# Layer 0 of a four-layer graph kernel: blocks of 512 query rows, four heads in turn for each tile, and layer seams worked block by block

## What is computed

```
layer 0: Q, K, V = h @ Qw + Qb, h @ Kw + Kb, h @ Vw + Vb          (8 heads)
         e[i,j,h]  = leaky_relu(S1[i, adj[i,j], h] + S2[j, adj[i,j], h], 0.2)
         out       = softmax_j(e) @ V per head, then @ Pw + Pb     (every j counts, adj picks the relation)
layer 1: hn = (h - mean(h)) / norm;  s = (hn @ w_k) @ (hn @ w_q)^T / sqrt(8)
         a  = adj * softmax(s), rows made to sum to 1;  (a + a^2/2 + a^4/6) @ hn
layer 2: Wh = h @ W;  e = leaky_relu(Wh a1 [i] + Wh a2 [j], 0.2)
         elu(softmax_j(e where adj > 0) @ Wh)
layer 3: a hyperbolic log-map summed over neighbours, then an exp-map
```

## Time and profile before

| | us |
|---|---|
| time, median of 3 executions | 1080.58 (1079.04 to 1087.63) |
| the profiled execution, its own time | 1082.16 |
| its span in the profile | 1079.9 |
| PE busy | 937.5 (87%) |
| DVE busy | 728.5 (67%) |
| POOL busy | 555.8 (51%) |
| ACT busy | 546.0 (51%) |

### The profile page before, as it was taken

One profiled execution on the slowest core, in us unless ns is written; L12 is line 12 of the kernel. 1 busy time (PEld: TensorE's weight loads), 2 busy tenths in 40 slices (PEclk: granted clock), 3 DMA queues, 4 the chain that ended last, 5 costly groups with the idle time before them and its releaser, 6 DMA issues.

```text
span 1079.9 us, 14479 instructions
## 1 busy us (share of the span) xinstructions
PE 937.5 (87%) x5239; PEld 336.0 (31%) x5239; DVE 728.5 (67%) x1145; ACT 546.0 (51%) x943; POOL 555.8 (51%) x658
## 2 busy tenths in 40 slices
PE   1996999999999999999996599999667939999970
PEld 1762222222222222222223522333262334555430
DVE  3145777777778777777774567411328667999987
ACT  0374666666665666656660076100100137899970
POOL 2006788898889888888870000000000007799962
PEclk8566999999999999999997579999857965999995
DMA  9472002021211121120000000000000000000000
GB/s 196 64 156 80 12 21 75 21 71 33 66 38 59 33 67 35 28 73 22 22 21 1 0 1 1 1 1 1 1 0 39 1 1 0 1 1 1 1 0 19
DMA packets 24940, 34.05 MB, mean 32 GB/s; under 512 B 16219, under 2 KB 16363, under 8 KB 23718
## 3 DMA queue, kind: packets, MB, share of 16 engines
q1 hardware_dynamic: 22566, 24.75, 7.9%
q0 software_dynamic: 2304, 8.39, 4.4%
HBM read 40.22 MB, written 1.30 MB: 38 GB/s over the span
## 4 chain that ended last, share of the span: by engine, by line
PE 72%; DVE 16%; issue 4%; DMA 3%; SPq 2%; ACT 1%; POOL 1%; DVEq 0%; ACTq 0%; POOLq 0%
PE ps L1074 22%; PE ps L1084 11%; PE ps L1181 8%; PE ps L1061 5%; DVE big L411 4%; PE ps L1053 4%; PE ps L1215 3%; PE ps L1155 3%; PE ps L1251 3%; DVE big L724 2%; DMA big<-in_L_gnn_Pw_dram 2%; DVE big L408 2%; PE ps L1145 2%; PE ps L938 1%; PE ps L1223 1%
## 5 line engine op out<-in xcount | busy, mean ns | idle before, releaser
L530 DVE COPY_PREDICATED big<-mask,ps 128x512 f32<-128x512 uint8 x512 | 338.2, 724 | 115.2 <-PE ps L1061 107.6
L368 POOL TENSOR_SCALAR big<-big 128x512 f32<-128x512 f32 x512 | 356.3, 713 | 72.5 <-PE ps L1084 72.2
L851 ACT ACTIVATE ps<-ps 128x512 f32<-128x512 f32 x512 | 266.8, 582 | 167.1 <-PE ps L1053 167.1
L1074 PE MATMUL ps<-big 128*64 128x512 f32 x1024 | 258.9, 613 | 0.0
L380 POOL TENSOR_TENSOR big<-big 128x512 f32<-128x512 f32 x40 | 67.3, 1684 | 342.1 <-ACT big L911 342.1
L1084 PE MATMUL ps<-big 128*32 128x512 f32 x1024 | 136.5, 605 | 0.0
L1053 PE MATMUL ps<-op_r,op_l 18*128 18x512 bf16 x512 | 110.3, 386 | 8.4 <-DMA op_r<-split_scratch 7.1
L1074 PEld LDWEIGHTS ps<-big 128*64 128x64 f32 x1024 | 58.6, 136 | 135.7 <-issue 98.4
L1251 PE MATMUL ps<-big 66*128 66x512 f32 x160 | 86.1, 668 | 2.2 <-DVE big L697 1.3
L411 DVE TENSOR_TENSOR big<-big,mask 128x512 f32<-128x512 f32 (+1 forms) x72 | 65.8, 933 | 12.8 <-ACT big L871 11.5
L1061 PE MATMUL ps<-op_r,op_l 9*128 9x512 bf16 x512 | 70.7, 390 | 2.0 <-ACT ps L851 2.0
(11 more groups left out here) (235 smaller groups left out, 1137.1 us busy)
## 6 DMA issues: line engine op xcount, KB each, us to landing
big<-max_scratch SPq DMA_DIRECT2D x9, 1024.0 KB, 4.9
big<-in_adj_dram POOLq DMA_DIRECT2D x16, 512.0 KB, 6.5
big<-rden_scratch SPq DMA_DIRECT2D x30, 256.0 KB, 3.3
op_l<-split_scratch SPq DMA_DIRECT2D x64, 36.0 KB
op_r<-split_scratch SPq DMA_DIRECT2D x64, 36.0 KB
x_nat<-in_x_dram SPq DMA_DIRECT2D x1, 512.0 KB, 4.1
out_dram<-x_nat SPq DMA_DIRECT2D x1, 512.0 KB, 3.8
den_scratch<-y_nat SPq DMA_DIRECT2D x30, 8.0 KB
```

The costliest lines, as they stand in the source:

```text
L368: pool.tensor_scalar(ring[:, k % RING, :], vrow[:, head % 2, i0:i0 + HALF], HUGE, g0[:, head, jt:jt + 1], ALU.min, ALU.max).then_inc(s["ba ...
L530: dve.copy_predicated(ring[:, k % RING, :], mask[:, jt, i0:i0 + HALF], ps[:, k % SLOTS, :])\
L851: act.activation(ps[:, k % SLOTS, :], ps[:, k % SLOTS, :], ACT.Relu, scale=-1.0).then_inc(s["relus"], 1)
L1074: m = pe.matmul(ps[w * D:(w + 1) * D, MAIN, :], vp[:, head, jt + w, :], ring[:, (u + w) % RING, :], start=(jt == 0), stop=(jt == NT - 2))
```

## The change

Layer 0 goes by blocks of 512 queries as the outer loop, with the heads in two groups of four (`GROUPS` is 8: block n // 2, heads 4 * (n % 2) and on). Within a group the tiles of four heads alternate for each key tile. A visit has two tiles, there are 256 of them, and `units(v)` is 3 * (v - 3) // 2. Five PSUM banks turn over for tiles and for 62 further pieces of work (`EXTRAS`), which take a bank in the same rotation: 24 halves of adj tiles (the prologue turns only 4 of the 16 tiles), 8 pairs of value rows for heads 4 to 7, and after each group its denominators and products turned to rows, where DVE scales them (`take_den`, `take_acc`) and POOL adds them to x (`add_shares`); after each block, layer 1's normalised rows, keys and queries (`hq`, `kqn`, `kqT`). The trips of the denominators through DRAM are gone. All operands of layer 0 are staged once, the first 16 DMAs by SP and ACT together; the splits leave in one DMA; `a_rel` is read in longer pieces, and adj waits for the weights. In the last round of layer 1 each block is normalised, transposed and multiplied as soon as it is there, and layer 2's row comes from a product and two ACT operations in place of DRAM.

```diff
-    PER_HEAD = BLOCKS * NT
-    SLOTS = 6
-    TRIO = 3
-    MAIN, DEN = 6, 7
-    BLKS = 4
-    NINE = PARTS * PARTS
-    STAGED = 16
+    QUAD = 4
+    GROUPS = H // QUAD * BLOCKS
+    SLOTS = 5
+    MAIN, DEN = 5, 7
+    PAIRS = PARTS * (PARTS + 1) // 2
+    ROWS = 2 * PARTS * PARTS
     NQ = 2 * REL * H
+    TB = HALF // P
...
-        TILES0 = H * PER_HEAD
-        BY_ROW = H * BLOCKS - 2
-        VISITS = -(-TILES0 // TRIO)
-        UNITS = TILES0 // 4 * 3
...
+        GROUP = NT * QUAD
+        TILES0 = GROUPS * GROUP
+        VISITS = TILES0 // 2
+        PER_GROUP = GROUP // 2
+        UNITS = TILES0 // QUAD * 3
 
         def units(v):
 
-            return min(max(9 * (v - 3) // 4, 0), UNITS)
-
-        def trio(v):
-
-            return range(TRIO * v, min(TRIO * v + TRIO, TILES0)) if 0 <= v < VISITS else ()
+            return min(max(3 * (v - 3) // 2, 0), UNITS)
...
+        def where(k):
+
+            n = k // GROUP
+            return n, n // 2 * HALF, n % 2, k % GROUP // QUAD, k % QUAD
...
+        for n in range(NT // 2):
+            extra(3 * n + 2, "val", n)
+        for n in range(2 * (NT - FIRST)):
+            extra(3 * n + 3 if n < 8 else 2 * n + 11, "adj", 2 * FIRST + n)
+        for n in range(GROUPS - 1):
+            for i, kind in enumerate(("den", "acc", "acc")):
+                extra((n + 1) * PER_GROUP + 6 + 2 * i, kind, n if kind == "den" else 2 * n + i - 1)
+        for q in range(BLOCKS - 1):
+            for i, kind in ((45, "hq"), (48, "kqn"), (58, "kqT")):
+                extra((2 * q + 2) * PER_GROUP + i, kind, q)
...
+        ORDER = []
+        for v in range(LAST):
+            ORDER += [("tile", k) for k in range(2 * v, 2 * v + 2) if k < TILES0] + EXTRAS.get(v, [])
+        ORDER += END
+        PLACE = {o: n for n, o in enumerate(ORDER)}
+
+        def slot(kind, arg):
+
+            return PLACE[kind, arg] % SLOTS
...
-                sp.dma_start(arel[:, r, :, :], a_rel[r, :, :].rearrange("(c p) h -> p c h", p=P))\
-                    .then_inc(s["a_in"], 16)
+                sp.dma_start(arel[:, r, :, :].rearrange("p (w c) h -> p w c h", w=2),
+                             a_rel[r, :, :].rearrange("(w p c) h -> p w c h", w=2, c=DC)).then_inc(s["a_in"], 16)
...
-            sp.wait_ge(s["split_copied"], 1)
-            for c in range(NQ * PARTS * NT // P):
-                sp.dma_start(split_d.rearrange("q c (t n) -> (q c t) n", n=P)[c * P:(c + 1) * P, :],
-                             splitT[:, c * P:(c + 1) * P]).then_inc(s["rows_out"], 16)
+            sp.wait_ge(s["split_copied"], 2)
+            sp.dma_start(split_d.rearrange("q c (t n) -> (q c t) n", n=P).rearrange("(b p) n -> p b n", p=P),
+                         splitT.rearrange("p (b n) -> p b n", n=P)).then_inc(s["rows_out"], 16)
...
             stage_row(0)
-            sp.wait_ge(s["rows_out"], 16 * (NQ * PARTS * NT // P))
-            for q in range(8):
-                stage_rows(0, q)
+            sp.wait_ge(s["rows_out"], 16)
+            for head in range(QUAD):
+                stage_left(head)
             stage_row(1)
-            for q in range(8):
-                stage_rows(1, q)
...
+            for head in range(QUAD, H):
+                stage_left(head)
+                stage_right(head)
+            for n in range(2, GROUPS):
+                sp.wait_ge(s["based"], (n - 1) * GROUP)
+                stage_row(n)
...
-        PROLOGUE = [("hT", 0), ("fold", 0), ("adj", 0), ("s", 0), ("adj", 1), ("value", 0), ("max", 0), ("adj", 2),
-                    ("value", 1), ("max", 1), ("adj", 3), ("value", 2), ("tab", 0), ("adj", 4), ("value", 3),
-                    ("adj", 5), ("value", 4), ("adj", 6), ("value", 5), ("max", 2), ("value", 6), ("value", 7)]
-        PROLOGUE += [x for t in range(7, NT) for x in [("adj", t)] + ([("value", t + 1)] if t + 1 < NT else [])]
+        PROLOGUE = [("w", 0), ("fold", 0), ("hT", 0), ("s", 0), ("adj", 0), ("adj", 1), ("max", 0), ("adj", 2), ("max", 1),
+                    ("value", 0), ("adj", 3), ("value", 1), ("adj", 4), ("tab", 0), ("value", 2), ("split", 0),
+                    ("adj", 5), ("value", 3), ("adj", 6), ("value", 4), ("adj", 7), ("value", 5), ("value", 6), ("value", 7)]
...
+            def load_adj(t):
+                pool.dma_start(ADJ_HOME[home(t)], adj_d[t * P:(t + 1) * P, :]).then_inc(adj_in[home(t)], 16)
+
+            pool.wait_ge(s["w_in"], 16 * 6)
+            for t in range(FIRST + 2):
+                load_adj(t)
...
+            pool.wait_ge(s["vp_read"], NT // 2)
+            pool.wait_ge(s["split_ready"], 1)
+            for head in range(QUAD):
+                scale_values(head)
+            pool.wait_ge(s["adj_turned"], 2 * FIRST)
...
+            for v in range(VISITS):
+                for k in range(2 * v, 2 * v + 2):
+                    select(k)
+                for kind, arg in EXTRAS.get(v, ()):
+                    if kind == "val":
+                        take_values(arg)
+                    elif kind == "den":
+                        take_den(arg)
+                    elif kind == "acc":
+                        take_acc(arg)
...
+                stage_right(head)
...
-            root(4)
+                    y_out(n, c)
+            for c in range(BLOCKS):
+                y_out(APPS - 1, c)
+                if c >= 2:
+                    hT_out(c - 2)
+                root(6 + c, slice(c * TB, (c + 1) * TB))
             act.preload_act_table_set("natural_log_exp_and_others")
-            copy_h(3, DA)
+            hT_out(2)
+            hT_out(3)
             act.wait_ge(s["tab_in"], 2)
-            act.activation(tab2[:, :, :], tab2[:, :, :], ACT.Exp).then_inc(s["tab_ready"], 1)
+            act.activation(tab2[:, 1:3, :], tab2[:, 1:3, :], ACT.Exp).then_inc(s["tab_ready"], 1)
+            for c in range(BLOCKS):
+                act.wait_ge(s["row_bc"], c + 1)
+                act.activation(ps[:, c, :], ps[:, c, :], ACT.Relu, bias=small[:, 40:41]).then_inc(s["relus"], 1)
+                act.wait_ge(s["relus"], TILES0 + c + 1)
+                act.activation(vrow2[:, c * HALF:(c + 1) * HALF], ps[:, c, :], ACT.Exp, scale=SLOPE - 1.0)\
+                    .then_inc(s["vrow2"], 1)
...
+            def free_slot(kind, arg):
+
+                n = PLACE[kind, arg] - SLOTS
+                if n >= 0:
+                    was, count = ORDER[n]
+                    pe.wait_ge(s[TAKEN[was][0]], count + TAKEN[was][1])
+                return slot(kind, arg)
 
...
             for v in range(LAST):
-                for k in trio(v - 1):
+                for k in range(max(2 * v - 2, 0), min(2 * v, TILES0)):
                     raise_floor(k)
-                for k in trio(v):
+                for k in range(2 * v, min(2 * v + 2, TILES0)):
                     cross(k)
+                for kind, arg in EXTRAS.get(v, ()):
+                    extra_work(kind, arg)
                 for u in range(units(v), units(v + 1)):
...
                 r.then_inc(s["y_turned"], 1)
 
+            def turn_h(c):
+
+                pe.wait_ge(s["hc_ready"], c + 1)
+                for t in range(c * TB, (c + 1) * TB):
+                    r = pe.transpose(ps[0:DA, c, t % TB * P:(t % TB + 1) * P], h[:, t, 0:DA], ident[:, :])
+                r.then_inc(s["hc_turned"], 1)
+
...
+            def row_scores(c):
+
+                pe.wait_ge(s["hTc_ready"], c + 1)
+                pe.matmul(ps[:, c, :], w2c[:, D:DA].to_broadcast([D, P]), hT[0:D, c * HALF:(c + 1) * HALF],
+                          start=True, stop=True).then_inc(s["row_bc"], 1)
```

More of the change, by code:

```diff
@@ new lines, in _ @@
+            q = BLOCKS - 1
+            take_den(GROUPS - 1)
+            take_acc(2 * GROUPS - 2)
+            take_acc(2 * GROUPS - 1)
+            of = quarter(q)
+            dve.wait_ge(s["acc_read"], 2 * GROUPS)
+            link(dve.reduce_sum(work[:, of, :], shares.rearrange("p t w d -> p t d w"), AX.X))
+            tt(x[:, of, :], x[:, of, :], work[:, of, :], ALU.add).then_inc(s["x_done"], 1)
+            for i in range(CENTER):
+                center_step(q, i)
+            dve.wait_ge(s["w_turned"], 2)
@@ L862, in _ @@
[L862 to L863 removed]
+                    act.activation(ps[:, slot("tile", k), :], ps[:, slot("tile", k), :], ACT.Relu, scale=-1.0).then_inc(s["relus"], 1)
+                for kind, arg in EXTRAS.get(v, ()):
+                    if kind == "adj":
+                        adj_out(arg, slot("adj", arg))
+                    elif kind == "hq":
+                        hq_out(arg)
+                    elif kind == "kqT":
+                        kq_out(arg)
@@ L1015, in maxima @@
                         .then_inc(s["mxb"], 1)
-                else:
+            for kind, t in PROLOGUE:
+                if kind == "w":
+                    weights()
+                elif kind == "fold":
+                    fold()
+                elif kind == "hT":
+                    features()
+                elif kind == "s":
```

(14 more changed lines are left out.)

844 lines of the change are left out of this document (470 added, 374 removed).

## The result

Slower, as forecast: 1104.97 us (median of 4 executions, 1104.71 to 1107.98) against 1079.81 for the kernel before in the same series, a ratio of 1.0227 with a 95% interval of 1.0172 to 1.0282. The forecast was 1108 in 1066 to 1132. The profiled execution took 1104.96 us, its span 1103.2.

A forecast was written before the change was run, and what follows sets the result against it. It took TensorE to bound the layer 0 loop. Changes of -24.2 (prologue), +94.0 (loop), -28.0 (layer 0 to 1) and -13.8 (layer 1 to 2, net) gave +28.0 on the span; forecast 1108 us, range 1066 to 1132.

The forecast's parts named there:

- The relu wait: Layer 0 loop: raises wait for both relus, 1.64 from cross to cross, so TensorE stands 0.31 in each of 128 short visits.
- the relu wait is hidden: Rival, chance 0.20: relus return within 1.33, so layer 0's loop is 31 us shorter, 1077 us in all.
- TensorE never stands in the loop: Rival, chance 0.14: relu and bank waits in layer 0 are both covered; loop 517 us, time 1049.
- The openings: Raises and crosses starting each layer 0 visit: on four different row bands they fall from 0.54 to 0.32 us.
- The pieces: The 62 further pieces in layer 0's loop: 29.9 us net work plus 28 us of bank waits.
- the term I had called the least certain: Waits of the 62 pieces for banks and copies in layer 0's loop: 28 us, bounds 0 and 50.
- The start and the end: Layer 0 loop: half-clock start and last units behind the last cross, 10 us.
- DVE falls behind: Rival, chance 0.14: DVE's steps hold TensorE's banks 0.3 more on some 90 visits and the half clock lasts: 1135 us.
- The prologue: Stretch before layer 0's loop: 68 us for 92.2, bounds 61 to 76.
- landed 3.9 later: Prologue: ScalarE's eight staging DMAs, issued by 65, land 3.9 us later, at 69.
- TensorE ends the values near 59: Prologue: TensorE finishes the values of heads 0 to 3 near 59 us; only then does ScalarE issue its staging DMAs.
- The seams: Layer 0 to 1: 21.5 us for 49.5; layer 1 to 2: 28.6 us for 44.7.

The follow-up runs named there:

- e2: The changed kernel with layer 0's relu over 256 of each tile's 512 columns, the rest left out: 1087.85 us, ratio 1.0079.
- e1: The kernel before with visits of two tiles and units in turns of one and two, six banks and head order kept: 1116.56 us, ratio 1.0294.
- e3: The changed kernel with the 62 pieces moved into short visits, none right behind a value pair: 1081.50 us, ratio 0.9973.
- e5: The changed kernel with the edits of e4 and e3 together: 1062.76 us, ratio 0.9775.
- e4: The changed kernel with `units(v)` rounded up, so units go two and one in turn: 1081.33 us, ratio 1.0017.
- e6: The changed kernel with each visit's crosses issued before the raises of the visit before: 1105.27 us, ratio 1.0253.
- e8: The changed kernel with SP's later staging (heads 4 to 7, second row of maxima) held until POOL has written eight bases: 1094.55 us, ratio 1.0163.
- e10: e5 with the one line of e8 added: 1052.02 us, ratio 0.9799.
- e11: e10 with SP also issuing the right halves of heads 0 and 1 in place of ScalarE: 1052.51 us, ratio 0.9801.

## Why the prediction was right, step by step

**The relu wait** was the step on which the sign hung, and it held: 1.61 and 2.33 measured, 1.64 and 2.33 forecast. The 1.64 came from the first visits by subtracting a relu and a clock difference; the measured path is 0.48 to the first relu, 1.07 for two, 0.05 to the second raise. e2 shows that the relu is the cause and e1 that the visit of two alone brings it. The rival *the relu wait is hidden* is refuted, and *TensorE never stands in the loop* with it: ScalarE is busy 314.04 of 569.30 us, 55%, and TensorE waits for it in each short visit that holds no piece. Room in volume says nothing of delay.

**The openings.** 0.32 for two raises and two crosses (the raises start at 225.24, the first product at 225.56) as worked out from the overlap of the earlier trace rows.

**The pieces** were forecast at 29.9 of work and 28 of bank waits on top of 128 x 3.97 = 508. Measured: 562.4 from first to last cross, less the 509.7 of e1, which has the same visits and no pieces, so 53 for both, or up to 57 by the count under e1, against 58. The waits at a group's start, forecast at 1.2 a group, can be read singly:

```profile
242.78 0.39 PE L1264 MATMUL ps<-op_r,op_l 18*128 18x512 bf16 x2
243.10 0.66 PE L1314 MATMUL ps<-ident,big 128*128 128x128 f32 x4
...
245.70 0.39 PE L1264 MATMUL ps<-op_r,op_l 18*128 18x512 bf16 x2
...
247.32 0.66 PE L1264 MATMUL ps<-op_r,op_l 18*128 18x512 bf16 x2
247.90 0.65 PE L1319 MATMUL ps<-ident,big 128*128 128x128 f32 x4
...
250.50 0.39 PE L1264 MATMUL ps<-op_r,op_l 18*128 18x512 bf16 x2
```

The den turn's visit takes 2.92, which is 2.33 and its work of 0.59. At the first acc the second cross is held (two crosses take 0.66 instead of 0.39): 3.18. The second acc has that and an own wait, 3.44, and the visit behind it 2.60. In all 1.05 over the work. The early adj halves behind a value pair wait 0.95 (98.20 - 96.93 - 0.32), as forecast. So the term I had called the least certain was near; it is also the one that is cheap to avoid, as e3 and e5 show.

**Where the loop was too dear by 7 us.** The steady visits: 128 x 3.94 = 504 for 508. The pieces: 53 for 58. The start and the end, forecast at 10: e1 has 509.7 - 504 = 5 for its slow-clock start and its block ends, and 640.5 - 633.6 = 7 lie behind the last cross, 12. The last rival, *DVE falls behind*, did not come, nor did its half clock: with PE busy 553.37 of 569.30 the granted clock was 0.99.

**The prologue was right by two errors.** The step *landed 3.9 later* was mis-sized: the earlier trace rows show 3.89 where only one head was staged, and the landing took 12.24 behind SP's seventeen further DMAs. The step *TensorE ends the values near 59* was as far off on the other side: the last copy of values ended at 52.76, so ScalarE issued from there. The result, 71.2 for 68, lies within its bounds, but the two steps were each 6 to 8 us off, and that they cancel is luck. So is some of the 71.2: in e3, whose prologue is the same, the last copy of values ended at 55.70 and the first cross came at 75.9. The granted clock from 29 to 52 us differs between executions: 0.65 in the changed kernel, e2 and e4, whose last copy ended at 52.8 to 53.0; 0.50 in e3, e6, e8 and e10, at 55.5 to 55.7; 0.70 and 0.72 in e5 and e11, at 54.4 and 54.8, so the clock in that stretch is not all of it. The splits, forecast to be landed by 53, were there at 44.7, but nothing on the way to the first cross waited for them. e8 is what the first cross does when the last landing is short: 2.72 for 3.9.

**The seams.** 21.7 for 21.5 and 28.1 for 28.6. Inside, DVE's sum of the shares took more than I gave it, and layer 2's start went as counted:

```profile
643.72 1.89 DVE L733 TENSOR_REDUCE work<-big 128x256 f32<-128x1024 f32 x1
...
654.12 1.86 PE L1329 MATMUL ps<-wkq,big 64*128 64x16 f32 x8 [0.77 <-ACT big L1013]
...
662.22 1.03 PE L1379 MATMUL ps<-hT 48*128 48x512 bf16 x2
```

```profile
821.46 5.42 PE L1420 MATMUL ps<-hT,w2c 64*128 64x512 f32 x6
...
838.15 6.07 DVE L812 SCALAR_TENSOR_TENSOR big<-big,mask 128x1024 f32<-128x1024 f32 x5 [1.08 <-ACT big L1084]
840.78 3.68 PE L1466 MATMUL ps<-big,y_nat 128*64 128x512 f32 x8 [6.40 <-DVE big L812]
```

Layer 2's row still costs 5.42 at TensorE's low clock. The chain of waits of the 28.1 has the last block's norm in it (815.3 to 817.7), then 1.28 of ScalarE's table load, TensorE's products and transposes with one copy between them (819.7 to 830.6), four times relu and exponential (833.4 to 838.1) and two of DVE's gates, 2.49. TensorE's part is the largest. No experiment was made on the seams; their account rests on these rows.

## What to carry to other kernels

When a loop's unit of work is made smaller, compare its length with the round trip that it has to cover, not the engines' shares of busy time: here a visit of 1.33 us of work had to cover 1.6 us from a cross through two relus, on an engine that was busy 55 to 60% of the time, and in e1 that cost 37 us. If the round trip can't be shortened, put what has to be done anyway into the visits that wait (e3; with two like products in a row, e5: 43.6 us), and keep work that takes a bank in the same rotation at a distance from its predecessor's release. Count which tile each bank is taken from: two pieces in one visit cost 5 us in e3 and e5, and with the other order of crosses and raises they deadlock. Hold back transfers that nobody needs yet while one is in flight that everybody waits for.
